# Gathering the first four groups of each edge layer inside the node chain before it

## What is computed

```
x = layernorm(x + L0(x, edge_weight1))                   # weighted sum, MLP
x = layernorm(x + L1(x, edge_attr_64))                   # sum, max, mean of attributes, MLP

# third layer
h      = relu(concat(x[src], x[dst]) @ W1 + b1)
inter  = h @ W2 + b2
gated  = inter * sigmoid(inter @ Wg + bg)
x = layernorm(x + segment_sum(gated, src) / max(count(src), 1))

# fourth layer
xl, xr = x @ W_l + b_l, x @ W_r + b_r
g      = leaky_relu(xl[src] + xr[dst] + edge_attr_16 @ W_e, 0.2)
alpha  = segment_softmax(einsum(g, att), dst)            # 4 heads of 16
out    = segment_sum(xl[src] * alpha, dst) + bias
x = layernorm(x + gelu(batchnorm(out) + x))
```

## Time and profile before

| | |
|---|---|
| median of 3 runs | 6424.94 us (6419.04 to 6425.12) |
| span of the profiled execution | 6445.0 us |
| busy: TensorE / VectorE / ScalarE / GpSimd | 54% / 58% / 27% / 55% |
| first node chain ends, `edges_3` begins (VectorE's first instruction) | 1469.05 us |
| `edges_3` | 1469 to 3757 us |
| second node chain | 3757 to 3914 us |
| `edges_4` | 3914 to 6321 us |
| `finish_4` | to the end |

### The profile page before, as it was taken

How to read it: one execution, slowest core, us unless ns; L and a number is a source line. 1 busy time by engine, 2 the same in 40 slices (tenths; PEclk the granted TensorE clock), 3 DMA queues, 4 the chain that set the end, 5 groups by cost and what they waited for, 6 DMA issues and landing times. The chain is left out here.

```text
span 6445.0 us, 56951 instructions
## 1 busy us (share of the span) xinstructions
PE 3469.2 (54%) x12150; PEld 1967.8 (31%) x12150; DVE 3716.2 (58%) x4303; ACT 1751.8 (27%) x3305; POOL 3538.9 (55%) x3662
## 2 busy tenths in 40 slices
PE   3565655573443344344444424677666766776772
PEld 2344433341222222222222212333333333333331
DVE  9988955552333333333333343777777777777776
ACT  1233323371111111111111111333333333333331
POOL 5430033326666666666666656666666666666653
PEclk8566667785666666666666655767777677667665
DMA  8756457713333334333333312333333333333331
GB/s 198 208 187 202 150 154 194 132 28 91 102 103 101 103 100 106 99 101 104 106 99 100 104 43 63 86 85 87 85 87 85 86 86 85 86 86 85 88 81 32
DMA packets 994791, 677.97 MB, mean 105 GB/s; under 512 B 645273, under 2 KB 798667, under 8 KB 993734
## 3 DMA queue, kind: packets, MB, share of 16 engines
q1 hardware_dynamic: 718424, 341.42, 21.1%
q0 software_dynamic: 116880, 124.33, 10.4%
q10 hardware_dynamic: 159390, 211.24, 9.7%
HBM read 344.06 MB, written 332.55 MB: 105 GB/s over the span
## 5 line engine op out<-in xcount | busy, mean ns | idle before, releaser
L1655 POOL DMA_INDIRECT got<-tabg,ix x1568 | 1481.5, 945 | 874.7 <-DMA t<-rows 427.9
L1461 POOL DMA_INDIRECT got<-tabg,ix x1568 | 1481.5, 945 | 788.2 <-issue 455.3
L182 PE MATMUL p_out<-ident,run 128*128 128x128 f32 (+1 forms) x3136 | 667.6, 360 | 410.4 <-ACT rows L1519 213.4
L1559 DVE TENSOR_TENSOR_SCAN own<-mk,own,p_first 128x512 f32<-128x512 bf16 x195 | 247.1, 1267 | 1100.0 <-remote 874.4
L182 PEld LDWEIGHTS p_out<-ident,run 128*128 128x128 f32 (+1 forms) x3136 | 547.3, 216 | 733.4 <-issue 599.5
L1481 PE MATMUL p_inter<-hid,W 128*128 128x512 f32 x392 | 313.5, 894 | 806.3 <-issue 676.9
L1790 DVE TENSOR_TENSOR_SCAN top<-p_reset,top,logit 128x512 f32<-128x512 f32 x195 | 249.6, 1280 | 537.3 <-ACT logit L1764 228.7
L168 PE MATMUL p_small<-ident,ea 128*32 128x128 f32 (+1 forms) x784 | 179.6, 376 | 690.7 <-ACT rows L1753 613.8
L1483 PE MATMUL p_gate<-hid,WF 128*128 128x512 f32 x392 | 293.3, 841 | 285.8 <-ACT gate L1513 148.1
L1528 ACT ACTIVATE hid<-pre,B 128x512 f32<-128x512 f32 x196 | 141.2, 720 | 1113.7 <-DVE pre L1575 797.2
L498 DVE TENSOR_TENSOR_SCAN run<-p_mk,run,feat 128x512 f32<-128x512 f32 x302 | 370.5, 1268 | 54.7 <-remote 32.8
(11 more groups left out here) (348 smaller groups left out, 6831.8 us busy)
## 6 DMA issues: line engine op xcount, KB each, us to landing
t<-rows ACTq DMA_DIRECT2D x195, 512.0 KB
first<-start SPq DMA_DIRECT2D x390, 256.0 KB
t<-rows ACTq DMA_DIRECT2D x195, 288.0 KB
got<-tabg,ix POOLq DMA_INDIRECT x3136
start<-zeros SPq DMA_DIRECT2D x100, 500.0 KB
ea<-in_ea_dram SPq DMA_DIRECT2D x390, 128.0 KB
mk<-marks SPq DMA_DIRECT2D x780, 64.0 KB
start<-zeros SPq DMA_DIRECT2D x195, 256.0 KB
```

Source lines behind the costliest of these rows:

```text
L182: mm = nc.tensor.transpose(bank[0:g.p, cc, :], by_place(t, g)[:, :, cc], ident[:, :])
L1461: nc.gpsimd.indirect_dma_start(got[s][0:g.p, cc, h, :], None, tabg, bass.IndirectOffsetOnAxis(ap=ix[0:g.p, g.n, h, cc:cc + 1], axis=0)).th ...
L1655: nc.gpsimd.indirect_dma_start(got[s][0:g.p, cc, h, :], None, tabg, bass.IndirectOffsetOnAxis(ap=ix[0:g.p, g.n, h, cc:cc + 1], axis=0)).th ...
```

## The change

`node_chain` gets the tiles `got` and the semaphores `got_in` of the coming edge layer with its indices, as `ahead`. Behind the fetch of `prime`, and behind a wait for the loads of the indices, GpSimd issues the gathers of groups 0 to 3, which the edge layer then leaves out; that begins with group 4 and waits until group 0 is turned. The tiles and semaphores belong to a stage `fetched` around chain and edge layer, for each of the two layers. For space, `wall` goes: L694 writes over `wprod`.

```diff
@@ build
-        node_chain(..., tabg[0], tabo[0], start2, tuple(index_loads(dsts, ix3)), ...)
-        edges_3(..., w2g, b2g)
-        node_chain(..., tabg[1], tabo[1], start3)
+        with Stage(nc) as fetched:
+            got, got_in = [sb(fetched, f"got{i}", [P, C, 2, D]) for i in range(AHEAD)], [sem(fetched, f"got_in{i}") for i in range(AHEAD)]
+            node_chain(..., tabg[0], tabo[0], start2, (ix3, got, got_in), tuple(index_loads(dsts, ix3)), ...)
+            edges_3(..., w2g, b2g, got, got_in)
         lasts = sb(ctx, "lasts", [P, NJ, T3])
-        edges_4(..., we, att)
+        with Stage(nc) as fetched:
+            got, got_in = [...], [...]
+            node_chain(..., tabg[1], tabo[1], start3, (ix4, got, got_in))
+            edges_4(..., we, att, got, got_in)
@@ Marks
-        nc.vector.scalar_tensor_tensor(out=self.wall[:, :], in0=self.wprod[:, :], ...
+        nc.vector.scalar_tensor_tensor(out=self.wprod[:, :], in0=self.wprod[:, :], ...
@@ new function
+def gather_group(nc, got, table, ix, g, got_in):
+    s = g.slot(AHEAD)
+    for cc in range(C):
+        for h in range(2):
+            nc.gpsimd.indirect_dma_start(got[s][0:g.p, cc, h, :], None, table,
+                                         bass.IndirectOffsetOnAxis(ap=ix[0:g.p, g.n, h, cc:cc + 1], axis=0)).then_inc(got_in[s], 16)
@@ node_chain, GpSimd, at its end
                 nc.gpsimd.indirect_dma_start(prime[:, :], ...).then_inc(primed, 16)
+                wait_from(pool, indexed, 16 * len(indices))
+                ix, got, got_in = ahead
+                for n in range(AHEAD):
+                    gather_group(nc, got, tabg, ix, Group(None, n), got_in)
@@ edges_3 and edges_4, GpSimd
-                def gather(g):
-                    s = g.slot(AHEAD)
-                    wait_from(pool, turned_got, g.n - AHEAD + 1)
-                    ... (the same eight gathers)
-                for n in range(NG + 1):
-                    gather(Group(None, n))
+                for n in range(AHEAD, NG + 1):
+                    pool.wait_ge(turned_got, n - AHEAD + 1)
+                    gather_group(nc, got, tabg, ix, Group(None, n), got_in)
```

More of the change, by code:

```diff
@@ L640, in __init__ @@
         if ew is not None:
-            self.wt, self.wrun, self.wprod, self.wall = (sb(c, n, [SR, SC]) for n in ("wt", "wrun", "wprod", "wall"))
+            self.wt, self.wrun, self.wprod = (sb(c, n, [SR, SC]) for n in ("wt", "wrun", "wprod"))
             self.crow = sb(c, "crow", [1, 2 * SR])
@@ L693, in weigh @@
         dve.wait_ge(self.walls, 2)
-        nc.vector.scalar_tensor_tensor(out=self.wall[:, :], in0=self.wprod[:, :], scalar=self.ccol[:, 0:1], in1=self.wrun[:, :],
+        nc.vector.scalar_tensor_tensor(out=self.wprod[:, :], in0=self.wprod[:, :], scalar=self.ccol[:, 0:1], in1=self.wrun[:, :],
                                        op0=ALU.mult, op1=ALU.add).then_inc(self.walls, 1)
@@ L947, in gather_rows, with node_chain @@
                                      bounds_check=E - 1, oob_is_err=False).then_inc(counted, 16)
+def gather_group(nc, got, table, ix, g, got_in):
[4 more added lines that the diff above has]
+                                         bass.IndirectOffsetOnAxis(ap=ix[0:g.p, g.n, h, cc:cc + 1], axis=0)).then_inc(got_in[s], 16)
 def bn(t, k, width=D):
     return t.unsqueeze(2).to_broadcast((P, k, width))
-def node_chain(nc, sb, ps, sem, X, info, info_next, key, nid, ident, prime, source, weights, biases, tabg, tabo, start, indices=(), mlp=None):
+def node_chain(nc, sb, ps, sem, X, info, info_next, key, nid, ident, prime, source, weights, biases, tabg, tabo, start, ahead, indices=(), mlp=None):
     width = 2 * D if mlp else D
@@ L1397, in _, with edges_3 @@
                         due(t, (FEW + 1, spread_2), (FEW + 5, biased_rows), (FEW + 2, scale_2), (FEW, pooled))
-def edges_3(nc, sb, ps, sem, ix, marks, tabg, start, prime, next_start, t2, ident, b2a, w2b, b2b, w2g, b2g):
+def edges_3(nc, sb, ps, sem, ix, marks, tabg, start, prime, next_start, t2, ident, b2a, w2b, b2b, w2g, b2g, got, got_in):
     MARKS, LAGS, ROUND = 8, 5, 8
@@ L1410, in edges_3 @@
         mk = [sb(c, f"mk{i}", [P, W], BF16) for i in range(MARKS)]
-        got = [sb(c, f"got{i}", [P, C, 2, D]) for i in range(AHEAD)]
         own, pre, hid, gate, run = ([sb(c, f"{n}{i}", [P, W]) for i in range(2)] for n in ("own", "pre", "hid", "gate", "run"))
@@ L1417, in edges_3 @@
         zeroed, weights_in, folds, folded = (sem(c, n) for n in ("zeroed", "weights_in", "folds", "folded"))
-        first_in, got_in = ([sem(c, f"{n}{i}") for i in range(AHEAD)] for n in ("first_in", "got_in"))
+        first_in = [sem(c, f"first_in{i}") for i in range(AHEAD)]
         mk_in = [sem(c, f"mk_in{i}") for i in range(MARKS)]
@@ L1577, in _, with edges_4 @@
                 each(dve, (4, multiply), (4, accumulate), (0, spread), (1, add))
-def edges_4(nc, sb, ps, sem, ix, ea16, marks, tabg, start, prime, t3, tops, lasts, ident, sel2, we, att):
+def edges_4(nc, sb, ps, sem, ix, ea16, marks, tabg, start, prime, t3, tops, lasts, ident, sel2, we, att, got, got_in):
     R = 2 * HEADS
@@ L1589, in edges_4 @@
         blocks = [sb(c, f"blocks{i}", [P, P]) for i in range(3)]
-        first, got = ([sb(c, f"{n}{i}", [P, C, 2, D]) for i in range(AHEAD)] for n in ("first", "got"))
+        first = [sb(c, f"first{i}", [P, C, 2, D]) for i in range(AHEAD)]
         ea = [sb(c, f"ea{i}", [P, C, 2, ED]) for i in range(AHEAD)]
@@ L1603, in edges_4 @@
         zeroed, made, weights_in = (sem(c, n) for n in ("zeroed", "made", "weights_in"))
-        first_in, got_in, mk_in = ([sem(c, f"{n}{i}") for i in range(AHEAD)] for n in ("first_in", "got_in", "mk_in"))
+        first_in, mk_in = ([sem(c, f"{n}{i}") for i in range(AHEAD)] for n in ("first_in", "mk_in"))
         stored, tops_out = ([sem(c, f"{n}{i}") for i in range(2)] for n in ("stored", "tops_out"))
```

17 lines of the change are left out of this document (7 added, 10 removed).

## The result

The changed kernel takes 6437.3 us (median of 20 runs, 6420.92 to 6451.31), the kernel before 6420.16 us beside it (20 runs): ratio 1.0028, 95% interval 1.0021 to 1.0035. It is slower by some 18 us (13 to 22), small, but just clear of the bound of 0.2% that the prediction set. The forecast was 6428.9 us and "within 0.2%"; the time lies in the range, on the side to which I had given 0.27. The time flatters the forecast: the kernel before came out 4.8 us lower here than in the runs that the forecast started from. The forecast for the change itself was +4.0 us, and that is 13 to 14 us short.

A forecast was written before the change was run, and what follows sets the result against it. GpSimd's gather issue, 1.25 us start to start, was taken as the bound. Third layer +5.7, fourth -2.8 and exits +1.1 made +4.0 us, which on the median 6424.94 gave 6428.9 us; range 6412 to 6446 us.

The forecast's parts named there:

- What bounds the kernel: Both edge layers: GpSimd's issue sets the pace, 1.25 us from gather to gather, 10.0 us a group, plus stops.
- The moved gathers: End of each node chain: 32 gathers after prime, uncovered, +40.0 us a joint; the added wait for index loads costs nothing.
- The flush behind them: GpSimd's DRAIN at each chain's end: 2.7 us behind the last gather instead of 8.2, giving back 5.4 us a joint.
- The start of the layers: Start of each edge layer: group 4 waits for group 0's turn, starting 16.7 us (third) and 10.1 us (fourth) in.
- Layers 3 and 4 from there: Both edge layers to their last groups at the old steady pace: third layer +5.7 us, fourth -2.8 us.
- The rest: Two added stage exits cost +1.1 us; the setup's overwritten operand and the tiles' new places cost nothing.
- The tail of prime: Rival, both joints: GpSimd's hidden work behind prime delays the first moved gather; +14.8 us, 6439.8 us; chance 0.17.
- The crawl: Rival, fourth layer's start: consumers stay slow, group 7 comes 81.7 us after the start; some +41, 6466 us; chance 0.08.
- The better rhythm: Rival, third layer: four groups between stops instead of three, lasting; -74.6 us, 6354 us in all; chance 0.08.
- The head start as meant: Rival, both layers: early fetch hides 4.34 us in the fourth, nothing in the third; -4, 6421 us; inside the forecast's chance.
- The chances: Whole kernel against the kernel before: within 0.2% (12.8 us) 0.60, slower 0.27, faster 0.13.

The follow-up runs named there:

- e7: The changed kernel with the 32 moved gathers placed ahead of the fetch of prime instead of behind it: 5600.59 us in one run, no changed kernel beside it.
- e11: The changed kernel, with GpSimd also waiting at the chain's end until the last moved group has landed: 5601.18 us in one run.
- e4: The changed kernel with only groups 0 and 1 moved for each layer, against the kernel before: ratio 0.9996.
- e1: The changed kernel again, unedited, for a second profile, against the kernel before on the same chip: 6488.65 against 6473.12 us, ratio 1.0031.
- e2: The kernel before again, unedited, for a second profile, against the kernel before: ratio 0.9998.
- e9: The changed kernel, unedited, on a chip without stops, against the kernel before: 5586.36 against 5561.21 us, ratio 1.0050.
- e3: The changed kernel's outer stage around chain and edge layer kept, but no group moved, against the kernel before: ratio 0.9998.
- e6: The changed kernel with one group moved for the third layer and three for the fourth, against the kernel before: ratio 1.0008.
- e8: The kernel before with eight gather tiles instead of four in the third layer, nothing moved, against the kernel before: ratio 1.0007.

## Why the prediction was right and wrong

**What bounds the kernel** was read rightly: GpSimd's issue, 1.25 us a gather. On the chips without stops it is the edge layers but for the 14 to 21 us behind the last gather.

**The moved gathers** cost their full 40.0 us at each joint, without cover, and the wait for the indices cost nothing: 0.30 us between prime and the first one.

**The flush behind them is the step that failed.** I took the DRAIN's 2.7 us from the end of the third layer, since it follows the same kind of instruction there, and 8.2 as the other bound. It measured 9.13 at both joints in all profiles of the change, outside both. Each layer starts 41.0 us late, not 34.6, and 2 x 6.4 = 12.8 us are missing from the sum: 4.0 + 12.8 = 16.8, against the 13 to 22 us measured. The choice went by likeness of the instruction, and e7 and e11 show that the length doesn't go by that, nor by landing. What it does go by stays open. At the joints it was 8.15 with 99 indirect DMAs since the DRAIN before, 8.81 with 107, 9.13 with 115, 123 and 131; at the layers' ends 7.91 with 1536, 8.56 with 1544, 9.21 with 1552, then 2.42 with 1560 and 2.75 with 1568, but 7.91 with 1568 and eight tiles. These lengths come back to 0.15 us in every profile, on both kinds of chip, so they go by the program, and no simple count gives them. Nothing here says what GpSimd does in a DRAIN.

**The start of the layers** held: group 4 at 16.7 and 9.6 us after the start, forecast 16.7 and 10.1. This is the core of the case. In the old order GpSimd issued groups 0 to 3 in the time that the layer needs anyway until group 0 is turned; moved ahead of the barrier, the same 40 us lie bare, and the wait that they covered lies bare behind them as idle time. The price by the number of moved groups has a kink: nothing but the longer DRAIN while what is left to issue is longer than that wait, then the whole of the difference. (With two groups on a chip with stops, e4, the third layer's group 4 came 4.3 us later than before, because TensorE's word was late; the time did not show it.) Group 4 in the third layer, on chips without stops: 50.9 us after prime with none moved, 51.5 with one, 58.4 with three, 67.7 with four; in the fourth 51.3, 52.3 with three, 60.6 with four.

**Layers 3 and 4 from there.** I had +5.7 and -2.8 at the last groups; with the missing 6.4 us they should be +12.1 and +3.6, and the pair of e1 and e2 has +11.8 and +7.5 there, and +9.6 and +5.9 at the exits. So the third layer gives back what I said, and the fourth, for which I had put 6.4 us, gives back 1.9 us by the last group and 3.6 by the exit; in single profiles such a difference is within the scatter. The first stop after the start came before group 8, with 6.0 us (in the first profile 1.3 before group 7 and 5.2 before group 8), where I had 4.7 before group 7. Old stops can be saved only where there are some: where GpSimd has none, the change costs 25 us (e9).

**The rest**: +1.1 us for the exits can't be told from nothing (e3).

**The rivals.** The tail of prime gave +14.8 us, next to the 18 measured, but by another mechanism: the first moved gather started 0.30 us behind prime, so nothing that ran on behind prime held it. What was lost is the DRAIN's gain: it was as long as before and 1.0 us more. The number came near by luck, because this rival also priced that gain as lost. The crawl did not come: in the fourth layer group 7 stands 44.1 us after the start (4002.00 - 3957.94), not 81.7. The better rhythm did not come (e1, e2). The head start as meant hid its 4.3 us in the fourth layer and no more; the rule of the Trainium skill ("DMA: Bandwidth & Descriptors", Rules for kernel authors) to issue a DMA early and wait for it late gives no more than that here, since it is the issue itself that bounds.

**The chances.** 0.27 for slower was too little. The sum of +4.0 stood close under a bound of +12.8, with one term taken at its favourable end at both joints; with the DRAIN left as it was (8.2), which nothing in the change shortens, the forecast would have been +14.8 and slower.

None of these versions is faster than the kernel before. The best, two groups for each layer or one and three, can't be told from it.

## What to carry to other kernels

Prefetching across a barrier pays only for what the new stage would wait for; ask first what the engine that issues does in the time that is set free. Here it was the bound of both stages, so its work moved from a place where it covered a wait to one where everybody waited for it. And where the length of a flush or barrier is not understood, take it as unchanged, and carry the hoped gain as a bound. The size of the loss is of these runs: 13 to 22 us where GpSimd also stops at its slots, 19 to 36 where it doesn't.

## What the chips showed that was not expected

**Two kinds of chip.** The same kernel before takes 6420 and 6473 us in two comparisons and 5556 and 5561 in two others, each group of comparisons on a chip of its own and at one time, so the difference may belong to the time and not to the chip. The difference stands in the edge layers: 11.6 and 12.1 us a group against 10.0. The windows of the two layers of the changed kernel (length, busy PE, PEld, DVE, ACT, POOL, granted clock, DMA share, GB/s), e1 and then e9:

```profile
1526.00:3785.70 2259.70, 925.29 (x3141) 533.47 (x3141) 745.75 (x790) 373.28 (x589) 1451.43 (x1536) 0.64 0.38 102
3987.50:6361.00 2373.50, 1641.51 (x5292) 857.45 (x5292) 1746.25 (x1966) 840.40 (x1764) 1452.12 (x1539) 0.70 0.37 85
```

```profile
1366.30:3315.90 1949.60, 1028.34 (x3141) 603.52 (x3141) 765.49 (x790) 379.23 (x589) 1451.47 (x1536) 0.72 0.44 118
3504.40:5453.70 1949.30, 1459.38 (x5292) 807.77 (x5292) 1727.12 (x1966) 829.19 (x1764) 1452.45 (x1539) 0.78 0.45 103
```

GpSimd and the DMAs do the same work in the same busy time. The mean granted clock of TensorE is lower in e1 (0.64 and 0.70 against 0.72 and 0.78), and whether that is a cause or comes of the waiting isn't shown; TensorE's own busy time is 103 us less there in the third layer and 182 us more in the fourth, while the layers are 310 and 424 us longer. What differs besides is how soon the others answer: in e9 TensorE turns a group right after its rows have come, VectorE adds it at once, and GpSimd goes on without a gap (timeline in the middle of the third layer):

```profile
2386.04 1.12 PE L175 MATMUL p_got<-ident,got 128*128 128x128 f32 x4 [4.67 <-DMA got<-tabg,ix]
2386.39 0.94 POOL L959 DMA_INDIRECT got<-tabg,ix  x1 [0.30 <-issue]
2387.25 0.69 DVE L1584 TENSOR_TENSOR pre<-own,p_got 128x512 f32<-128x512 f32 x1 [4.56 <-PE p_got L175]
```

The median from the end of a group's last gather to its turn in the third layer is 3.4 us on this kind of chip (e6, e8) and 21.5 us on the other (before, e1, e2). The data are not what is late: in the DMA record the last packet of a gather ends 1.2 us behind the gather's recorded end in the median, in the kernel before on the first kind of chip, and 1.3 us in e8 on the other. So the late signals of the earlier trace rows are no trait of the kernel, and where they are missing the bound is GpSimd's issue alone. Why one chip delays them and another doesn't, these runs don't show.

**A DRAIN of 9.13 us on an idle GpSimd** with the rows of its last gathers landed (e11), paid by every engine where GpSimd is the last to reach the barrier, as at both joints. At the layers' ends it is hidden: in the changed kernel it ends at 3738.3, and the layer's exit comes at 3757.
